# A graph layer and an inverted bottleneck in one kernel: transpose moved up, two images per loop turn, last taps as GpSimd products added by DMA

## The chip, the core and the metric

The kernel runs on one core of a Trainium2 chip. Its engines are TensorE (PE in the profile: matmuls; PEld is its loading of weights), VectorE (DVE), ScalarE (ACT), GpSimd (POOL) and SyncE (SP), which issues DMAs. The engines run their own instruction streams in order and meet through semaphores. The metric is the time of one execution on the device in microseconds; lower is better.

## The reference

The input `x` is 16 images of 96 channels and 64 x 64 pixels, float32. Layer 0 is a graph layer over windows of 8 x 8 pixels; layer 1 is a 1x1 convolution to 576 channels, a depthwise 3x3 convolution and a 1x1 convolution back.

```
y = affine(conv1x1(x, fc1_w, fc1_b), fc1_s, fc1_t)
nodes = windows of y: 64 nodes with 96 features each
idx = the 9 nearest nodes by the distance of normalised features
feat = concatenate([x_i, x_j - x_i])
h = max over the 9 neighbours of gelu(affine(feat @ ew.T + eb))
x = affine(conv1x1(h, fc2_w, fc2_b), fc2_s, fc2_t) + x      # layer 0
h = relu(bn(w1 @ x))                                        # 96 -> 576
h = relu(bn(depthwise 3x3 of h, nine taps per channel))
x = x + bn(w2 @ h)                                          # 576 -> 96
```

## The kernel before

The unit of layer 0 is a pair of windows, 128 nodes; an image has 32 pairs (`p`), 4 to a chunk of 8 rows, and the run has 512 (`P`). The unit of layer 1 is a strip of 16 rows, four to an image, with the 576 channels in four full groups of 128 and a half group (`gr` 0 to 4). One strip is done in the time of 8 pairs; it follows the chunks of layer 0 by two strips. Everything is laid out by hand: for each engine a function `image` runs over the pairs of an image, and its text is the order of the instructions. The images -1, 0, 15 and 16 (starts and ends) are written out, and images 1 to 14 are a hardware loop, one image per turn (`image_loop`).

Within pair `p` the engines do, for layer 0:

- TensorE: `scores` of pair P+3, `gather` part 0 of P, `expand` of P+1 (the one-hot matrix of neighbour offsets, into `pvu`), `feature_transpose` of P+2 (the offsets, transposed into `pself`), `gather` part 1, `self_full`, `values` of P+1 (into `pvu` again), `gather` part 2, `self_half`. Between them stand the shared jobs (`misc_jobs`: fc1, ssq, inv, fc2, w1, w2), which take turns in three banks `pmisc`.
- ScalarE: `gelu` part 0 of P, `onehot` of P+1 (from `pvu` to `MV`), `featT_copy` of P+2, `gelu` part 1, `vu_copy` of P+1 (from `pvu` to `VU`), `feature_square` of P+3, `gelu` part 2, `gelu_self`, with the evacuations of the shared jobs between them; at the pair's end `tap0` and `relu2` of layer 1 where the tables say so.
- VectorE: `largest`, `indices` and `feature_a` of P+3, `maxima` of P-1, and between them the taps.
- GpSimd: the norms, copies of `xn` to `xs`, and two kinds of accumulating DMA (`add_input` and `add_x1`).

Waits that the change touches: `self_full` waits for `featT_evac` of P+2, since both live in one bank; `feature_transpose` waits for `self_gelu` of the pair before it and for `feat_ready`; `values` waits for `onehot_ready`; `gather` part 0 waits for `vu_evac`.

The depthwise convolution of a group is nine taps into `acc`: `tap0` on ScalarE (it writes), taps 1 to 8 on VectorE (multiply and add, `hpad` and `acc` in, `acc` out), then `relu2` on ScalarE and w2 on TensorE. `TAP_AT` gives each of the 8 slots of a strip its taps; a slot `o` falls on pairs with p = o modulo 8. The taps of the half group have 512 columns, the others 1024.

Of the kernel before, what the change touches and what calls it, by code (L numbers as in the profile page):

```python
# [4 lines left out]
B, C, H, W = 16, 96, 64, 64  # L5
# [37 lines left out]
TAP0_LATE = {0: [0], 1: [1], 2: [2], 4: [3]}  # L43
RELU2_AT = {6: [0], 7: [1], 10: [2], 11: [3, 4]}
W2_AT = {12: 0, 13: 1, 14: 2, 16: 3}
TAP_COUNTS = [5, 4, 4, 6, 4, 5, 6, 6]
# [3 lines left out]
FIRST = [(g, k) for k in range(1, TAPS) for g in (0, 1)]  # L50
SECOND = [(g, k) for k in range(1, TAPS) for g in (2, 3, 4)]
# [107 lines left out]
def tap_number(s, g, k):  # L159

    k -= 1
    return s * 5 * (TAPS - 1) + (2 * k + g if g < 2 else 2 * (TAPS - 1) + 3 * k + g - 2) + 1
# [7 lines left out]
def build(nc, x, p97, p128, rows97, consts, consts128, consts16, out):  # L170
# [3 lines left out]
    with ctx:  # L174
# [26 lines left out]
        def col97(k):  # L201
# [45 lines left out]
        acc = sb("acc", [128, 2, 5, STRIP * W])  # L247
        res = sb("res", [C, 2, CW])
# [25 lines left out]
            "vu_ready", "vu_evac", "gather_ready", "self_ready", "gelu_done", "self_gelu"))  # L274
        sp_passed, pool_passed, dve_passed = sem("sp_passed"), sem("pool_passed"), sem("dve_passed")
# [5 lines left out]
        def image_loop(eng, image, tail):  # L281

            image(-1, 16, PAIRS)
            image(0, 0, PAIRS)
            with eng.Fori(1, B - 1) as b:
                image(b, 0, PAIRS)
            image(B - 1, 0, PAIRS)
            image(B, 0, tail)
# [63 lines left out]
        def _(pool):  # L352
# [10 lines left out]

            def add_x1(b, p, o, t, s, q):

                fb, fp = when(b, p, 1)
                pool.wait_ge(misc_evac, job_at(fb, fp, "w2", q))
                pool.sem_inc(pool_passed, 1)
                c = 2 * t + q // 2
                nc.gpsimd.dma_start(res[:, q // 2, :], x1v[:, c * CW:(c + 1) * CW],  # L370
                                    accum_op=ALU.add).then_inc(out_sum[q // 2], 16)
# [33 lines left out]
            def image(b, p0, p1):  # L405
                for p in range(p0, p1):
                    h = 1 if p < 16 else 0
                    bi = b if h else b + 1
                    if p % 16 == NORMS_AT and valid(bi, B):
                        inverse_norms(b, p, bi, h)  # L410
                    for o, t, s, q in due_in(ADD_AT, b, p):
                        add_x1(b, p, o, t, s, q)
                    if p % 16 in XN_AT and valid(bi, B):
                        stationary_copy(bi, 4 * h + XN_AT[p % 16])
                    if p % 4 == 1:
                        bc, c = (b, (p - 5) // 4) if p >= 5 else (b - 1, CHUNKS - 1)
                        if valid(bc, B):
                            add_input(b, p, bc, c)
# [5 lines left out]
        def _(pe):  # L424
# [168 lines left out]
            def image(b, p0, p1):  # L593
                for p in range(p0, p1):
# [7 lines left out]
                    if valid(P, NPAIRS):  # L602
# [4 lines left out]
                        gather(P, p, 0)  # L607
                    for k in part_of(jobs, 0):
                        shared_job(b, p, k, jobs[k])
                    if valid(P + 1, NPAIRS):  # L610
                        expand(P + 1, p + 1)
                    if valid(P + 2, NPAIRS):
                        feature_transpose(P + 2, p + 2)
# [19 lines left out]
        def _(act):  # L633
            def shared_evac(b, p, k, job):
# [37 lines left out]
                elif kind == "w1":  # L672
                    t, s, (gr, m) = job[1:]
                    if m == 0:

                        if due(count := tap_number(s - 1, gr, TAPS - 1)):
                            act.wait_ge(tap_done, count)
                    sc, sh = sc1[:, gr:gr + 1], sh1[:, gr:gr + 1]
# [98 lines left out]
            def relu2(s, par, gr):  # L777
                if due(count := tap_number(s, gr, TAPS - 1)):
                    act.wait_ge(tap_done, count)
# [10 lines left out]
            def image(b, p0, p1):  # L790
                for p in range(p0, p1):
# [7 lines left out]
                    if valid(P, NPAIRS):  # L799
                        gelu(P, p, 0)  # L800
                    for k in part_of(jobs, 0):
# [6 lines left out]
                    if valid(P + 2, NPAIRS):  # L808
                        featT_copy(P + 2, p + 2)
# [255 lines left out]
```

## Time and profile before

| What | Value |
|---|---|
| Median of 3 runs | 4372.47 us (4371.74 to 4379.67) |
| Profiled execution | 4362.46 us |
| Its span | 4360.7 us |
| Mean granted TensorE clock | 0.99 |
| PE busy | 4041.2 us, 26688 matmuls |
| DVE busy | 4081.9 us, 5296 instructions |
| ACT busy | 3606.4 us, 7141 instructions |
| POOL busy | 503.2 us, 548 instructions |

The span is the profiled execution from its first to its last instruction. Busy times are unions, so instructions that overlap by some tens of ns on one engine count once. PE, DVE and ACT overlap almost everywhere, and their order in time is what the rows further down are for.

### The profile page before, as it was taken

Reading aid. Unit: us, or ns where it says so; the run is one execution under the profiler, and the core shown is the slowest. Engines: PE = TensorE matmul, PEld = TensorE weight load, DVE = VectorE, ACT = ScalarE, POOL = GpSimd, SP = SyncE. Lnnn points to the kernel's source line nnn. Section 1 sums busy time; section 2 is a strip of 40 time slices with the busy share of each in tenths; the row PEclk is TensorE's granted clock in tenths of the full one; section 3 lists DMA queues with packets and bytes.
Section 4 is the critical chain, followed back from the end, with each engine's and each line's share of the span. In section 5 each row is a group of like instructions: output and inputs, shape, how many; then the busy total and the mean of one; then the engine's idle time right before and its main releaser. Section 6 shows DMA issues by size and latency. Waiting matters only on the chain.

```text
span 4360.7 us, 84229 instructions
## 1 busy us (share of the span) xinstructions
PE 4041.2 (93%) x26688; PEld 2406.4 (55%) x26688; DVE 4081.9 (94%) x5296; ACT 3606.4 (83%) x7141; POOL 503.2 (12%) x548
## 2 busy tenths in 40 slices
PE   4999999999999999999999999999999999999994
PEld 2555555555555555555555555555555555555552
DVE  2599999999999999999999999999999999999998
ACT  3788888888888888888888888888888888888883
POOL 0011111011111011011111010111010111010100
PEclk9999999999999999999999999999999999999997
DMA  1111120111111111121111111111111111201111
GB/s 47 23 30 32 25 45 18 33 38 32 33 30 28 29 36 34 25 44 19 33 36 33 33 26 24 37 33 33 30 33 25 38 32 25 45 18 25 30 21 24
DMA packets 53036, 134.61 MB, mean 31 GB/s; under 512 B 7778, under 2 KB 9058, under 8 KB 46372
## 3 DMA queue, kind: packets, MB, share of 16 engines
q0 software_dynamic: 28672, 50.35, 8.1%
q1 hardware_dynamic: 23876, 78.22, 6.7%
q8 instruction: 250, 4.10, 0.4%
q14 instruction: 238, 1.95, 0.2%
HBM read 77.68 MB, written 25.69 MB: 24 GB/s over the span
## 4 chain that ended last, share of the span: by engine, by line
PE 66%; issue 11%; DVE 11%; ACT 11%; DMA 0%; SPq 0%; ACTq 0%; DVEq 0%; POOL 0%; POOLq 0%
PE pg L567 15%; PE pmisc L493 8%; PE pg L570 8%; DVE acc L949 8%; PE pvu L554 7%; PE pmisc L477 5%; PE pself L581 5%; ACT MV L741 4%; PE pmisc L438 3%; PE pmisc L460 2%; PE pmisc L462 2%; PE pmisc L445 2%; PE pvu L540 2%; ACT hpad L688 2%; PE pmisc L495 2%
## 5 line engine op out<-in xcount | busy, mean ns | idle before, releaser
L949 DVE SCALAR_TENSOR_TENSOR acc<-hpad,w,acc 128x1024 f32<-128x1024 f32 (+1 forms) x2560 | 2919.5, 1174 | 66.1 <-ACT acc L774 66.1
L567 PE MATMUL pg<-MV,VU 128*128 128x512 f32 x2048 | 1148.0, 643 | 22.6 <-ACT VU L749 21.0
L758 ACT ACTIVATE g<-pg 128x512 f32<-128x512 f32 x1536 | 916.3, 597 | 147.5 <-PE pg L570 90.2
L936 DVE TENSOR_REDUCE hid<-g 128x192 f32<-128x1728 f32 x512 | 995.5, 1944 | 0.0
L741 ACT ACTIVATE MV<-pvu,cst 64x512 f32<-64x512 f32 x1024 | 694.8, 678 | 9.9 <-PE pvu L540 0.3
L477 PE MATMUL pmisc<-x,w 96*128 96x384 f32 (+1 forms) x1536 | 567.9, 481 | 18.4 <-ACT hpad L688 18.4
L570 PE MATMUL pg<-MV,VU 128*64 128x512 f32 x2048 | 530.3, 595 | 0.0
L493 PE MATMUL pmisc<-acc,w 128*96 128x256 f32 x2048 | 492.3, 384 | 31.3 <-ACT acc L781 31.3
L688 ACT ACTIVATE hpad<-pmisc,sh,sc 128x384 f32<-128x384 f32 (+1 forms) x768 | 482.4, 660 | 25.0 <-DVE acc L949 15.7
L477 PEld LDWEIGHTS pmisc<-x,w 96*128 96x128 f32 x1536 | 294.1, 192 | 326.0 <-issue 229.1
L581 PEld LDWEIGHTS pself<-MV,VU 128*128 128x128 f32 x2048 | 283.3, 191 | 335.7 <-issue 314.6
L493 PEld LDWEIGHTS pmisc<-acc,w 128*96 128x96 f32 x2048 | 334.8, 165 | 228.7 <-issue 122.5
L554 PE MATMUL pvu<-wVU,y 97*64 97x192 f32 x4096 | 447.9, 340 | 1.7 <-ACT MV L741 1.7
L581 PE MATMUL pself<-MV,VU 128*128 128x64 f32 x2048 | 308.3, 273 | 141.9 <-ACT featT L727 138.3
L749 ACT ACTIVATE VU<-pvu 128x384 f32<-128x384 f32 x512 | 250.9, 490 | 192.0 <-PE pvu L554 189.4
L781 ACT ACTIVATE acc<-acc,shd,scd 128x1024 f32<-128x1024 f32 (+1 forms) x320 | 358.0, 1142 | 24.4 <-DVE acc L949 24.4
L567 PEld LDWEIGHTS pg<-MV,VU 128*128 128x128 f32 x2048 | 309.4, 191 | 61.2 <-issue 30.4
L774 ACT ACTIVATE acc<-hpad,w 128x1024 f32<-128x1024 f32 (+1 forms) x320 | 334.2, 1044 | 0.0
L587 PEld LDWEIGHTS pself<-MV,VU 128*64 128x64 f32 x2048 | 145.4, 135 | 296.8 <-issue 296.8
L540 PEld LDWEIGHTS pvu<-featT,c 128*128 128x128 f16 x4096 | 186.0, 100 | 181.0 <-issue 156.5
L554 PEld LDWEIGHTS pvu<-wVU,y 97*64 97x64 f32 x4096 | 249.2, 136 | 55.6 <-ACT MV L741 2.0
L403 POOL COPY xs<-xn 96x512 f32<-96x512 f32 x128 | 159.5, 1247 | 1034.1 <-DVE xn L930 1034.1
(95 smaller groups left out, 4125.3 us busy)
## 6 DMA issues: line engine op xcount, KB each, us to landing
xin<-in_x_dram SPq DMA_DIRECT2D x32, 768.0 KB, 5.5
invb<-rows_dram SPq DMA_DIRECT2D x32, 768.0 KB
x<-in_x_dram POOLq DMA_DIRECT2D x128, 192.0 KB, 3.6
res<-x POOLq DMA_DIRECT2D x128, 192.0 KB, 3.6
out_dram<-res SPq DMA_DIRECT2D x128, 192.0 KB, 2.1
g<-in_consts_dram SPq DMA_DIRECT2D x1, 640.0 KB
w<-in_p_dram SPq DMA_DIRECT2D x1, 618.5 KB
rows_dram<-norm_rows SPq DMA_DIRECT2D x32, 16.0 KB, 1.4
```

The lines of the kernel that those rows point to most:

```text
L477: last = nc.tensor.matmul(ps[:, o:o + (hi - lo) * W], w1T[:, gr * 128:(gr + 1) * 128], x1[:, lo:hi, :], start=True, stop=True)
L493: nc.tensor.matmul(ps[0:C, 0:4 * W], w2T[:, gr, :], acc[:, par, gr, q * 4 * W:(q + 1) * 4 * W], start=(gr == 0), stop=False)
L554: last = nc.tensor.matmul(pvu[h:h + 64, O * w:O * (w + 1)], nodes, wVU[:, k, :], start=True, stop=True)
L567: last = nc.tensor.matmul(ps[:, :], VU[:, r, part, 0:ONE128], cols[part], start=True, stop=True)
L570: last = nc.tensor.matmul(ps[64 * w:64 * w + 64, :], VU[:, r, w, ONE128:O], cols[w], start=True, stop=True)
L581: nc.tensor.matmul(pself[:, 64 * w:64 * w + 64], VU[:, r, w, 0:ONE128], MV[:, r, w, KN * NODES:], start=True, stop=True)
L688: nc.scalar.activation(hpad[:, gr, r0:r1, 1:W + 1], ps[:, o:o + (r1 - r0) * W].rearrange("p (row col) -> p row col", col=W), ACT.Relu, bia ...
L741: last = nc.scalar.activation(MV[h:h + 64, p % 2, w, 0:KN * NODES].rearrange("p (n k) -> p n k", k=KN), pone[h:h + 64, :, :].rearrange("p ...
L758: nc.scalar.activation(g[:, p % 2, part, :, 0:KN], pg[(3 * p + part) % 2][:, :].rearrange("p (n k) -> p n k", k=KN), ACT.Gelu).then_inc(ge ...
L781: nc.scalar.activation(acc[:, par, gr, 0:n], acc[:, par, gr, 0:n], ACT.Relu, bias=shd[:, gr:gr + 1], scale=scd[:, gr:gr + 1]).then_inc(rel ...
L936: nc.vector.tensor_reduce(hid[:, c % 2, j, :, :], g[:, r], op=ALU.max, axis=AX.X).then_inc(hid_ready, 1)
L949: nc.vector.scalar_tensor_tensor(out=dst, in0=src, scalar=wk, in1=dst, op0=ALU.mult, op1=ALU.add).then_inc(tap_done, 1)
```

## The change

It has three parts. The transposed offsets: `feature_transpose` of pair P+2 stands directly behind `gather` part 0 on TensorE, and `featT_copy` directly behind `gelu` part 0 on ScalarE. The loop: a turn holds two images, and there are 7 turns. The taps: tap 8 of each of the four full groups leaves VectorE. GpSimd computes it as a product into a new buffer `tapped` (two halves, used in turn), and an accumulating DMA adds it to `acc` once taps 0 to 7 are there. `relu2` of these groups waits for that DMA, and the evacuation that overwrites `hpad` waits for the product too. The taps are spread anew over the slots (36 a strip, before 40), and `tap0` of group 3 moves from slot 4 to slot 3.

```diff
-TAP0_LATE = {0: [0], 1: [1], 2: [2], 4: [3]}
+TAP0_LATE = {0: [0], 1: [1], 2: [2], 3: [3]}
 RELU2_AT = {6: [0], 7: [1], 10: [2], 11: [3, 4]}
 W2_AT = {12: 0, 13: 1, 14: 2, 16: 3}
-TAP_COUNTS = [5, 4, 4, 6, 4, 5, 6, 6]
+TAP_COUNTS = [5, 4, 5, 4, 5, 4, 5, 4]
+PRODUCT_AT = {2: 0, 3: 1, 6: 2, 7: 3}
+SUM_AT = {5: (0, 1), 9: (2, 3)}
...
-FIRST = [(g, k) for k in range(1, TAPS) for g in (0, 1)]
-SECOND = [(g, k) for k in range(1, TAPS) for g in (2, 3, 4)]
+FIRST = [(g, k) for k in range(1, TAPS - 1) for g in (0, 1)]
+SECOND = [(2, 1), (3, 1), (2, 2), (3, 2), (4, 1), (2, 3), (3, 3), (4, 2), (2, 4), (3, 4), (4, 3), (2, 5), (3, 5), (4, 4),
+          (2, 6), (3, 6), (2, 7), (3, 7), (4, 5), (4, 6), (4, 7), (4, 8)]
...
+        tapped = sb("tapped", [128, 2, STRIP * W])
...
-            with eng.Fori(1, B - 1) as b:
+            with eng.Fori(1, B - 2, 2) as b:
                 image(b, 0, PAIRS)
+                image(b + 1, 0, PAIRS)
...
+            def tap_product(b, p, o, s, gr):
+
+                fb, fp = when(b, p, o - w1_slot(gr, 2))
+                pool.wait_ge(misc_evac, job_at(fb, fp, "w1", (gr, 2)))
+                pool.sem_inc(pool_passed, 1)
+                if due(count := 16 * (s if gr < 2 else s + 1)):
+                    pool.wait_ge(tap_sum[(gr + 2) % FULL], count)
+                pool.sem_inc(pool_passed, 1)
+                nc.gpsimd.tensor_scalar(tapped[:, gr % 2, :].rearrange("p (row col) -> p row col", col=W),
+                                        hpad[:, gr, 2:2 + STRIP, 2:2 + W], wd[:, gr, TAPS - 1:TAPS], None,
+                                        ALU.mult).then_inc(product_done, 1)
+
+            def add_product(t, s, gr):
+
+                pool.wait_ge(product_done, FULL * s + gr + 1)
+                pool.sem_inc(pool_passed, 1)
+                pool.wait_ge(tap_done, last_tap(s, gr))
+                pool.sem_inc(pool_passed, 1)
+                nc.gpsimd.dma_start(acc[:, t % 2, gr, :], tapped[:, gr % 2, :],
+                                    accum_op=ALU.add).then_inc(tap_sum[gr], 16)
...
                         gather(P, p, 0)
+                    if valid(P + 2, NPAIRS):
+                        feature_transpose(P + 2, p + 2)
                     for k in part_of(jobs, 0):
                         shared_job(b, p, k, jobs[k])
                     if valid(P + 1, NPAIRS):
                         expand(P + 1, p + 1)
-                    if valid(P + 2, NPAIRS):
-                        feature_transpose(P + 2, p + 2)
...
+                        if gr < FULL and due(count := FULL * (s - 1) + gr + 1):
+                            act.wait_ge(product_done, count)
...
             def relu2(s, par, gr):
-                if due(count := tap_number(s, gr, TAPS - 1)):
-                    act.wait_ge(tap_done, count)
+                if gr < FULL:
+                    act.wait_ge(tap_sum[gr], 16 * (s + 1))
+                else:
+                    act.wait_ge(tap_done, last_tap(s, gr))
...
                         gelu(P, p, 0)
+                    if valid(P + 2, NPAIRS):
+                        featT_copy(P + 2, p + 2)
...
-                    if valid(P + 2, NPAIRS):
-                        featT_copy(P + 2, p + 2)
```

The order on the engines at three places follows; the line numbers of the changed kernel are some 37 to 41 higher for the same instruction.

TensorE in pair 14 of an image in the loop, before: `scores` (pscore), `gather` (pg), the job w2 (acc,w), `expand` (featT,c), the transpose (c,feat), `self_full` (pself from MV,VU) and `values` (wVU,y).

```order
L517 MATMUL pscore<-xn,xs 64x64 x2
L519 MATMUL pscore<-c 64x64 x2
L562 ISA
L567 MATMUL pg<-MV,VU 128x512
L430 REGISTER_ALU
L493 MATMUL pmisc<-acc,w 96x256 x4
L495 MATMUL pmisc<-acc,w 96x256
L540 MATMUL pvu<-featT,c 128x64 x8
L530 MATMUL pself<-c,feat 128x64
L567 MATMUL pg<-MV,VU 128x512
L581 MATMUL pself<-MV,VU 128x64 x2
L554 MATMUL pvu<-wVU,y 64x192 x4
```

The same pair after the change:

```order
L554 MATMUL pscore<-xn,xs 64x64 x2
L556 MATMUL pscore<-c 64x64 x2
L599 ISA
L604 MATMUL pg<-MV,VU 128x512
L567 MATMUL pself<-c,feat 128x64
L467 REGISTER_ALU
L530 MATMUL pmisc<-acc,w 96x256 x4
L532 MATMUL pmisc<-acc,w 96x256
L577 MATMUL pvu<-featT,c 128x64 x8
L604 MATMUL pg<-MV,VU 128x512
L618 MATMUL pself<-MV,VU 128x64 x2
L591 MATMUL pvu<-wVU,y 64x192 x4
```

The transpose has moved from behind `expand` to ahead of the job; the rest keeps its order.

ScalarE at the end of pair 3 (and 11, 19, 27), before: the `VU` copy, the square of `feat`, the last two gelus, and `relu2` (acc from acc) of groups 3 and 4.

```order
L749 ACTIVATE VU<-pvu 128x384
L731 REGISTER_ALU
L732 ACTIVATE feat<-feat 128x16
L753 REGISTER_ALU
L758 ACTIVATE g<-pg 128x64x8
L764 ACTIVATE g<-pself 128x192
L781 ACTIVATE acc<-acc,shd,scd 128x1024
L781 ACTIVATE acc<-acc,shd,scd 128x512
```

The same place after the change:

```order
L788 ACTIVATE VU<-pvu 128x384
L770 REGISTER_ALU
L771 ACTIVATE feat<-feat 128x16
L792 REGISTER_ALU
L797 ACTIVATE g<-pg 128x64x8
L803 ACTIVATE g<-pself 128x192
L813 ACTIVATE acc<-hpad,w 128x1024
L822 ACTIVATE acc<-acc,shd,scd 128x1024
L822 ACTIVATE acc<-acc,shd,scd 128x512
```

`tap0` of group 3 (acc from hpad) now stands ahead of the two `relu2`; it has left the end of the next pair.

GpSimd in pair 1 of an image in the loop, with what each instruction waits for, before: a sum of x1 and the input chunk.

```order
L285 ISA
L370 DMA res<-x 96x512 [waits misc_evac]
L359 REGISTER_ALU
L361 ISA [waits misc_evac]
L361 DMA x<-in_x_dram 96x512
```

The same pair after the change, and the two products of pairs 2 and 3 behind it:

```order
L391 ISA [waits product_done]
L393 DMA acc<-tapped 128x1024 [waits tap_done]
L389 REGISTER_ALU
L391 REGISTER_ALU [waits product_done]
L393 DMA acc<-tapped 128x1024 [waits tap_done]
L399 ISA
L402 DMA res<-x 96x512 [waits misc_evac]
L370 REGISTER_ALU
L372 ISA [waits misc_evac]
L372 DMA x<-in_x_dram 96x512
L381 ISA [waits misc_evac]
L383 TENSOR_SCALAR tapped<-hpad,w 128x1024 [waits tap_sum2]
```

Two sums of products come first, and the two older DMAs queue behind them; the product behind waits until the first of these sums has landed.

## Rows read from the trace of the kernel before

**Rows 1.** The page, busy us, share of the span, instructions

```profile
PE 4041.2 (93%) x26688; PEld 2406.4 (55%) x26688; DVE 4081.9 (94%) x5296; ACT 3606.4 (83%) x7141; POOL 503.2 (12%) x548
```

**Rows 2.** Waits of the whole run: us in total, times, longest us

```profile
ACT VU L749 <- PE pvu L554: 189.4, 248, 1.4
...
PE pself L581 <- ACT featT L727: 138.3, 200, 2.1
...
ACT feat L732 <- DVE feat L919: 32.1, 47, 11.0
...
PE pscore L517 <- issue: 26.3, 13, 2.3
...
PE pmisc L460 <- DVE hid L936: 14.4, 15, 4.1
```

**Rows 3.** Windows: start:end length, busy us by engine, clock, DMA share, GB/s

```profile
1890.21:1956.86 66.65, 65.84 (x440) 39.99 (x438) 63.04 (x82) 58.34 (x117) 7.44 (x10) 1.00 0.19 39
1956.86:2019.95 63.09, 58.79 (x398) 34.80 (x396) 61.72 (x82) 54.18 (x110) 8.31 (x9) 1.00 0.13 24
...
1923.71:1933.84 10.13, 10.13 (x67) 6.58 (x65) 10.13 (x13) 8.05 (x17) 0.92 (x2) 1.00 0.00 0
1979.60:1988.54 8.94, 7.71 (x55) 4.41 (x53) 8.94 (x13) 7.76 (x17) 1.42 (x1) 1.00 0.00 0
...
2118.01:2127.41 9.40, 8.66 (x57) 5.26 (x55) 9.40 (x13) 6.75 (x13) 2.29 (x3) 1.00 0.05 5
```

**Rows 4.** Timeline of pair 14: start us, length us, what, idle time before

```profile
2001.68 1.36 ACT L741 ACTIVATE MV<-pvu,cst 64x512 f32<-64x512 f32 x2
...
2003.07 0.22 ACT L727 ACTIVATE featT<-pself 128x64 f16<-128x64 f32 x1
...
2003.43 0.63 PE L581 MATMUL pself<-MV,VU 128*128 128x64 f32 x4 [0.96 <-ACT featT L727]
...
2003.99 0.87 PE L554 MATMUL pvu<-wVU,y 97*64 97x192 f32 x8
...
2004.92 0.49 ACT L749 ACTIVATE VU<-pvu 128x384 f32<-128x384 f32 x1 [1.14 <-PE pvu L554]
```

**Rows 5.** Waits in the stretch 123 to 181 us, first image, no taps yet

```profile
PE pself L581 <- ACT featT L727: 8.6, 8, 1.2
```

**Rows 6.** Timeline at the start of pair 17

```profile
2021.30 0.52 ACT L764 ACTIVATE g<-pself 128x192 f32<-128x192 f32 x1
...
2021.91 1.02 PE L438 MATMUL pmisc<-xin,w 96*96 96x512 f32 x2
```

**Rows 7.** Timelines of VectorE and GpSimd where copies run

```profile
157.64 0.61 POOL L403 COPY xs<-xn 96x512 f32<-96x512 f32 x1 [5.28 <-DVE xn L930]
157.69 0.58 DVE L919 SCALAR_TENSOR_TENSOR feat<-idx,cst 128x16 f16<-128x16 uint32 x1
...
1977.54 1.28 DVE L949 SCALAR_TENSOR_TENSOR acc<-hpad,w,acc 128x1024 f32<-128x1024 f32 x1
1977.89 1.40 POOL L403 COPY xs<-xn 96x512 f32<-96x512 f32 x1 [14.95 <-DVE xn L930]
1978.74 0.09 DVE L909 MATCH_VALUE_LOAD idx<-top,pscore 128x8 f32 x1
...
2003.18 0.88 POOL L403 COPY xs<-xn 96x512 f32<-96x512 f32 x1 [5.54 <-DVE xn L930]
```

**Rows 8.** Groups by form: count, busy us, mean ns of one, idle before

```profile
L774 ACT ACTIVATE acc<-hpad,w 128x1024 f32<-128x1024 f32 x256 | 287.8, 1124 | 0.0
...
L919 DVE SCALAR_TENSOR_TENSOR feat<-idx,cst 128x16 f16<-128x16 uint32 x512 | 88.0, 172 | 0.7
```

**Rows 9.** The page, DMA: queue's packets, MB, share; issue's KB, us to landing

```profile
q0 software_dynamic: 28672, 50.35, 8.1%
...
res<-x POOLq DMA_DIRECT2D x128, 192.0 KB, 3.6
```

**Rows 10.** Timeline of VectorE at the end

```profile
4246.22 95.18 DVE L949 SCALAR_TENSOR_TENSOR acc<-hpad,w,acc 128x1024 f32<-128x1024 f32 x88
```

More of the change, by code:

```diff
@@ L159, in tap_number, with last_tap @@
 def tap_number(s, g, k):
-    k -= 1
-    return s * 5 * (TAPS - 1) + (2 * k + g if g < 2 else 2 * (TAPS - 1) + 3 * k + g - 2) + 1
+    return s * len(FIRST + SECOND) + (FIRST + SECOND).index((g, k)) + 1
+def last_tap(s, g):
+    return tap_number(s, g, TAPS - 2 if g < FULL else TAPS - 1)
 def due(count):
@@ L274, in build @@
             "vu_ready", "vu_evac", "gather_ready", "self_ready", "gelu_done", "self_gelu"))
+        product_done = sem("product_done")
+        tap_sum = [sem(f"tap_sum{k}") for k in range(FULL)]
         sp_passed, pool_passed, dve_passed = sem("sp_passed"), sem("pool_passed"), sem("dve_passed")
@@ L410, in image @@
                         inverse_norms(b, p, bi, h)
+                    for o, t, s, groups in due_in(SUM_AT, b, p):
+                        for gr in groups:
+                            add_product(t, s, gr)
                     for o, t, s, q in due_in(ADD_AT, b, p):
                         add_x1(b, p, o, t, s, q)
+                    for o, t, s, gr in due_in(PRODUCT_AT, b, p):
+                        tap_product(b, p, o, s, gr)
                     if p % 16 in XN_AT and valid(bi, B):
@@ L674, in shared_evac @@
                     if m == 0:
-                        if due(count := tap_number(s - 1, gr, TAPS - 1)):
+                        if due(count := last_tap(s - 1, gr)):
                             act.wait_ge(tap_done, count)
+                        if gr < FULL and due(count := FULL * (s - 1) + gr + 1):
+                            act.wait_ge(product_done, count)
                     sc, sh = sc1[:, gr:gr + 1], sh1[:, gr:gr + 1]
```

## Prediction

> **What bounds the kernel now.** I read the page first [rows 1]: TensorE is busy for 93% of the span, VectorE for 94% and ScalarE for 83%, so no engine has much room, and the averages can't say which of them the others wait for. The list of waits over the whole run can [rows 2]. Three things stand in it. TensorE waits 138.3 us in `self_full` for ScalarE's copy `featT`, and 26.3 us in 13 turns of the loop. ScalarE waits 189.4 us for `pvu`, which TensorE fills in `values`. And hardly anybody waits for VectorE: ScalarE 32.1 us for `feat` (part of it while the kernel starts), TensorE 14.4 us for `hid`. VectorE is full, but it seldom holds anyone up.
>
> Then I cut one image into pairs, from one `VU` copy to the next, and read the busy time of each stretch [rows 3]. The first line is the strip of pairs 1 to 8, the second that of pairs 9 to 16; the load differs because fc1 and ssq fall on pairs 1 to 6. In the first strip TensorE is busy 65.84 of 66.65 us: it is TensorE's. In the second it is busy 58.79 of 63.09 us, VectorE 61.72. Pair 5 (third line) is TensorE's without a gap, 10.13 of 10.13 us, and leaves ScalarE 2 us of room. Pair 12 (fourth line) takes 8.94 us though TensorE has 7.71 and ScalarE 7.76 of work.
>
> Pair 14 shows the mechanism [rows 4]. The one-hot activation (L741) ends at 2003.04, `featT` (L727) at 2003.29, and only then does `self_full` start, at 2003.43, after 0.96 us of idling; `values` can start at 2003.99, and ScalarE itself idles 1.14 us until `pvu` is full. Both engines stand still in one ring. Where ScalarE doesn't idle before the `VU` copy, the same wait of TensorE costs nothing: ScalarE is then the bound.
>
> **The change part by part.** All sums are made against the profiled execution, 4362.46 us; the median of the runs shown is 10.0 us more, which I add at the end.
>
> *Loop turns.* 14 turns become 7, each with the same work in it twice, so 7 branches back go. Each cost TensorE 26.3 / 13 = 2.02 us [rows 2], with nothing beside it in a pair that is TensorE's: **-14.1 us**. From 0 (if the longer body stalls on its own) to -14.
>
> *Transpose and `featT` early.* `self_full` no longer waits; the ring now closes from the one-hot's end to `values`. The one-hot comes 0.14 us later (TensorE does the transpose first, or ScalarE the copy), and TensorE starts 0.14 us after ScalarE's end as it did at 2003.43: 2003.04 + 0.14 + 0.14 = 2003.32 against 2003.99, so 0.67 us are won where both engines idle. That is in pairs 14 and 30 of each image, 31 in all: **-20.8 us**. In the first image, before the taps begin, almost every pair looks like this (8 waits of about 1.1 us in a stretch of 58 us [rows 5]); some 12 such pairs give **-8.0 us**. In pairs 11, 15, 27 and 31 `self_full` waits too, but ScalarE goes from work to work: 0.
>
> The price lies in `feature_transpose` itself. It waits for `self_gelu` of the pair before, and stands now right behind `gather` 0, where nothing covers it. In [rows 6] that activation (L764) ends at 2021.82, and TensorE goes on behind its gather at 2021.91; with the 0.14 us from above the transpose starts at 2021.96, 0.05 us late. Queued behind it are all of TensorE's jobs of the pair. In about nine of sixteen pairs, those that [rows 3] cut this way show as TensorE's, this is lost: 0.05 x 9 x 32 = **+14.4 us** (from 0 to 0.14 us each, +40).
>
> *`tap0` of group 3 from pair 4 to pair 3.* Seen between `VU` copies, about 1.0 us of ScalarE (L774, 1.12 us [rows 8] less the overlap with its neighbour) moves from the stretch of pair 5, in which it has room, into the stretch of pair 4 (and 12, 20, 28), which holds `relu2` of groups 3 and 4 as well. There the one-hot comes 1.0 us later, and 0.14 us from the edit before. In pair 4 `values` then starts about 0.4 us late, in pair 20 about 0.25; in pair 12 this eats what the early `featT` gives. Over 15 images **+9.8 us** (from 0 to +30).
>
> *Four full taps a strip leave VectorE.* A full tap takes 1.20 us from its start to the next one's (1977.54 to 1978.74 in [rows 7]): 4.8 us of some 62 us a strip. What this is worth is what others wait for VectorE, in the main part of the run in pairs 28 and 29 (9.40 us for 8.66 us of TensorE's work, last line of [rows 3]) and ScalarE's 0.4 us in pair 12, which the moved `tap0` takes: 0.9 x 15 = **-13.5 us**. The bounds are 0 and all waits on VectorE in [rows 2], -46 us.
>
> *The products on GpSimd.* No product of this size stands in the trace; the nearest row is the copy of 96x512 [rows 7]. It took 0.61 us with VectorE quiet (157.64), and 1.40 us when a tap ran as it came. VectorE pays as well: the small `feat` instruction beside the copy took 0.58 us, against a mean of 172 ns [rows 8]. So one holds the other up for as long as it runs. A product has twice the columns: between 0.6 us (no cost per column) and twice the 0.88 us of a half-covered copy (2003.18), 1.76 us; I take 1.1 us, the quiet copy and as much again less its fixed part. It costs VectorE nothing while `maxima` runs (nearly 2 of some 8 us) and up to 1.1 us in a row of taps, so at most 4.4 us of the 4.8 come back as stalls. I cost that at nothing in the body: VectorE then has 61.72 - 4.8 + 4.4 = 61.3 us in the strip of 63.09, and the first two products fall on the pair that keeps only four half taps. The cover is gone at 1.2 us a product.
>
> The Trainium skill has this as a rule (SBUF — State Buffer, "Who interferes with whom"): a VectorE instruction with two SBUF inputs and a GpSimd instruction that reads SBUF exclude each other for the whole instruction. The trace agrees, by 0.58 us against 172 ns. GPSIMD Engine Reference, "Elementwise — side-by-side cycle accounting", gives 1.03 cycles an element where a port is the limit; by it a product would be an estimated 0.9 us, and the sum the same.
>
> *The sums by DMA.* POOL issues 256 transfers more. In 28672 packets the queue's present transfers used 8.1% of the engines; those of 192 KB took 3.6 us to land [rows 9], so I expect 5 to 7 us for 512 KB. `relu2` comes more than ten us after the issue in every slot. Queued behind the sums on POOL are `add_x1`, the input chunk and the next product; the chunk is used two pairs later. Cost 0. Late next, were a sum 20 us under way, would be `relu2` of group 1 and w2 behind it.
>
> *The end.* After the last `maxima` VectorE runs 88 taps in 95.18 us with nobody beside it [rows 10]. After the change there are 77, with 12 full ones fewer and one half more: -13.6 us. Eight products break in, at 0.75 us: +6. The last sum lands about 3 us after the last tap, where now three `relu2` follow at once: +3. **-4.6 us.**
>
> Sum: -14.1 - 20.8 - 8.0 + 14.4 + 9.8 - 13.5 - 4.6 = -36.8; 4362.5 - 36.8 + 10.0 = **4336 us**, 0.8% faster.
>
> **The rivals.**
> 1. *TensorE becomes the only bound.* If my view that ScalarE holds pairs 11, 12 and 15 is wrong, and VectorE does by keeping everything late, then strips shrink to TensorE's busy time, 65.84 and 58.79 us: 5.1 us a pair of strips, 30 of them, -153, with the loop -167: about 4205 us. For it: VectorE's 94%, and 61.72 of 63.09 us. Against it: the short list of waits on VectorE.
> 2. *The product holds VectorE too long, and the kernel is slower.* Place: VectorE's row of taps in pairs 9 to 16. At 1.76 us a product, four cost 7.0 us for 4.8 won, VectorE needs 63.9 us where it needed 61.72, and the 32 such strips lose 2.2 us each, +70; the 13.5 are lost and the end pays 8 more: about 4428 us. It decides from 1.2 us a product.
> 3. *No change.* The transpose waits 0.14 us instead of 0.05: +26, which makes 4362 us; with the moved `tap0` at its upper bound as well, +20 more, 4382 us. The old 4372 lies between. For it: the order only moves a wait within one ring. Against it: in pair 14 both engines of the ring idle.
>
> **How the numbers follow.** Forecast, 20 to 85 us faster: 0.52. Rival 1: 0.18. Rival 3: 0.14. Slower, rival 2 or the upper ends of rival 3: 0.16. A measurement tells some 0.2% (9 us) from nothing, so faster 0.70, same 0.14, slower 0.16. The likeliest case alone spans 4290 to 4352. The range for 8 in 10 leaves out the lower half of rival 1 and the upper half of rival 2: 4245 to 4390.
>
> **What the profile after would show.** Right: no wait of `self_full` on `featT`, instead short ones of the transpose and of `values` on the one-hot; 6 loop waits near 2 us; VectorE's busy share down to 88 to 92%; products near 1.1 us without, 2 us with a tap before them; TensorE about as busy in us as now; pair 4 longer, the start of `values` in pair 14 some 0.7 us earlier in its pair. Wrong: VectorE's share stays at 94% with stretched taps (rival 2); TensorE idles below 2% between images 1 and 14 (rival 1); `relu2` waits on a sum; the second half of a turn stalls for instructions.

## The result and the profile after

The changed kernel took 4389.49 us (median of 6 runs, 4387.09 to 4391.21), the kernel before 4372.10 us beside it (6 runs, 4365.06 to 4379.67). The ratio is 1.0038, with a 95% interval of 1.0026 to 1.0051: 0.38% slower. The forecast was 4336 us; 4389.5 lies just inside the upper end of the range, on the side that was given 16%. The profiled span went from 4360.7 to 4385.9 us.

The page of the changed kernel, as in [rows 1]:

```profile
PE 4098.3 (93%) x26688; PEld 2418.2 (55%) x26688; DVE 3891.9 (89%) x5040; ACT 3623.8 (83%) x7141; POOL 1575.7 (36%) x1060
```

VectorE is 190 us less busy, GpSimd 1072 us more, and TensorE, with the same matmuls, 57 us more. The last is the first sign: a matmul whose weights are still being loaded counts as busy (below, in pair 17, the transpose's record starts at 2026.38, and its weights are in at 2026.45).

The waits of the whole run (us in total, times, longest), beside [rows 2]:

```profile
PEld pself L567 <- issue: 283.8, 448, 1.7
...
ACT VU L788 <- PE pvu L591: 135.2, 224, 1.7
...
PEld pself L567 <- ACT feat L771: 80.5, 64, 2.2
...
ACT feat L771 <- DVE feat L960: 69.2, 81, 11.2
...
PE pvu L591 <- ACT MV L780: 36.9, 92, 1.5
...
PE pscore L554 <- issue: 11.0, 6, 2.1
```

The wait of `self_full` on `featT` (138.3 us) has gone, and the 13 turns are 6. In their place stands a weight load, that of the transpose (L567): TensorE's loader stood idle before it 448 times. And ScalarE waits twice as long for VectorE's `feat`. The strips of image 7, cut as in [rows 3], first strip, second strip, pair 12:

```profile
1892.74:1960.89 68.15, 67.21 (x440) 40.09 (x438) 61.09 (x79) 58.70 (x117) 25.49 (x18) 1.00 0.35 67
1960.89:2024.41 63.52, 59.79 (x398) 35.06 (x396) 58.28 (x78) 54.27 (x109) 22.88 (x16) 1.00 0.30 59
1983.47:1992.99 9.52, 7.26 (x51) 4.13 (x47) 9.52 (x13) 8.71 (x18) 1.48 (x2) 1.00 0.00 0
```

The strip that is TensorE's grew from 66.65 to 68.15 us, the other from 63.09 to 63.52 though VectorE has 3.44 us less work in it. In pair 12 TensorE has work for 7.26 us and the pair takes 9.52 (8.94 before). Pair 14 did what was forecast; the rows that answer to [rows 4]:

```profile
2004.29 0.22 ACT L766 ACTIVATE featT<-pself 128x64 f16<-128x64 f32 x1
...
2006.51 1.37 ACT L780 ACTIVATE MV<-pvu,cst 64x512 f32<-64x512 f32 x2
2007.11 0.56 PE L618 MATMUL pself<-MV,VU 128*128 128x64 f32 x4
...
2007.93 0.87 PE L591 MATMUL pvu<-wVU,y 97*64 97x192 f32 x8 [0.27 <-ACT MV L780]
...
2008.85 0.49 ACT L788 ACTIVATE VU<-pvu 128x384 f32<-128x384 f32 x1 [0.35 <-PE pvu L591]
```

`featT` is ready before the one-hot even starts, and `values` follows the one-hot's end (2007.88) by 0.05 us.

### The profile page after: what moved, and what is told of

The parts are those of the page before. It is cut to its first block, busy times and chain, and to the rows that moved or that the text cites. A ratio compares the mean times of both kernels' runs of the same rounds, so it can differ in the third digit from the quotient of the medians.

```text
span 4385.9 us, 86104 instructions
## 1 busy us (share of the span) xinstructions
PE 4098.3 (93%) x26688; PEld 2418.2 (55%) x26688; DVE 3891.9 (89%) x5040; ACT 3623.8 (83%) x7141; POOL 1575.7 (36%) x1060
## 3 DMA queue, kind: packets, MB, share of 16 engines
q0 software_dynamic: 65536, 184.58, 23.8%
## 4 chain that ended last, share of the span: by engine, by line
PE 63%; ACT 14%; issue 12%; DVE 8%; DMA 1%; SPq 0%; DVEq 0%; ACTq 0%; POOL 0%; POOLq 0%
PE pg L604 15%; PE pmisc L530 8%; PE pg L607 7%; PE pvu L591 7%; PE pmisc L514 7%; DVE acc L990 6%; ACT MV L780 4%; PE pmisc L497 3%; PE pself L618 3%; PE pmisc L482 3%; PE pmisc L499 2%; PE pmisc L475 2%; PE pmisc L532 2%; ACT hpad L727 2%; ACT acc L822 2%
## 5 line engine op out<-in xcount | busy, mean ns | idle before, releaser
L990 DVE SCALAR_TENSOR_TENSOR acc<-hpad,w,acc 128x1024 f32<-128x1024 f32 (+1 forms) x2304 | 2726.2, 1208 | 244.3 <-ACT acc L813 241.7
L383 POOL TENSOR_SCALAR tapped<-hpad,w 128x1024 f32<-128x1024 f32 x256 | 831.1, 3318 | 10.5 <-DMA acc<-tapped 7.1
L393 POOL DMA_DIRECT2D acc<-tapped x256 | 229.6, 898 | 1534.9 <-DVE acc L990 1467.3
L514 PE MATMUL pmisc<-x,w 96*128 96x384 f32 (+1 forms) x1536 | 580.4, 490 | 17.3 <-ACT hpad L727 12.8
L727 ACT ACTIVATE hpad<-pmisc,sh,sc 128x384 f32<-128x384 f32 (+1 forms) x768 | 485.1, 663 | 15.9 <-POOL tapped L383 8.3
L514 PEld LDWEIGHTS pmisc<-x,w 96*128 96x128 f32 x1536 | 280.1, 191 | 260.0 <-issue 161.2
L435 POOL COPY xs<-xn 96x512 f32<-96x512 f32 x128 | 175.6, 1372 | 585.8 <-DVE xn L971 585.8
L618 PEld LDWEIGHTS pself<-MV,VU 128*128 128x128 f32 x2048 | 304.6, 191 | 116.9 <-issue 54.1
```

Source lines behind the costliest of these rows:

```text
L383: nc.gpsimd.tensor_scalar(tapped[:, gr % 2, :].rearrange("p (row col) -> p row col", col=W), hpad[:, gr, 2:2 + STRIP, 2:2 + W], wd[:, gr, ...
L514: last = nc.tensor.matmul(ps[:, o:o + (hi - lo) * W], w1T[:, gr * 128:(gr + 1) * 128], x1[:, lo:hi, :], start=True, stop=True)
L727: nc.scalar.activation(hpad[:, gr, r0:r1, 1:W + 1], ps[:, o:o + (r1 - r0) * W].rearrange("p (row col) -> p row col", col=W), ACT.Relu, bia ...
L990: nc.vector.scalar_tensor_tensor(out=dst, in0=src, scalar=wk, in1=dst, op0=ALU.mult, op1=ALU.add).then_inc(tap_done, 1)
```

## The experiments

The runs fall into three groups, each with its own runs of the kernel before (13, 13 and 10; medians 4367.28, 4367.18 and 4371.52 us); every ratio is to those of its group. Kernels of different groups are best compared by their ratios.

### The three parts one at a time

**Transpose and `featT` early, alone.** The kernel before with the move below in TensorE's `image`, and that of `featT_copy` to behind `gelu` 0 in ScalarE's, as in the change:

```diff
+                    if valid(P + 2, NPAIRS):
+                        feature_transpose(P + 2, p + 2)
                     for k in part_of(jobs, 0):
...
                         expand(P + 1, p + 1)
-                    if valid(P + 2, NPAIRS):
-                        feature_transpose(P + 2, p + 2)
```

> The kernel before with the transpose and the featT copy moved up, and nothing else. What I now hold (A): it wins 0.7 us in pairs 14 and 30 and 8 us in the first image, and loses 0.2 to 0.25 us in every pair that is TensorE's, because the weights of the transpose can't be loaded under the gather: all in all within 15 us of the kernel before, 4357 to 4380. The forecast on record: -14 us. Rival (B), the transpose is what made the change slower: 15 us or more slower than before.

Measured: 4383.20 us, ratio 1.0034 (1.0021 to 1.0047). Slower by itself, by 15.9 us: outside the 4357 to 4380 us of A, and at the near edge of B.

**Two images per turn, alone:**

```diff
-            with eng.Fori(1, B - 1) as b:
+            with eng.Fori(1, B - 2, 2) as b:
                 image(b, 0, PAIRS)
+                image(b + 1, 0, PAIRS)
```

> The kernel before with two images to a loop turn, and nothing else. Forecast and A: 7 waits of about 2 us fewer, 12 to 17 us faster. Rival: the longer body stalls on its own, within 5 us of before.

Measured: 4352.26 us, 0.9963 (0.9950 to 0.9976): 15.0 us faster, where 14.1 were forecast.

**Products, sums, tables and the moved `tap0`, alone:** the changed kernel with those two parts undone.

> The kernel before with the products on GpSimd, their sums by DMA, the new tap tables and tap0 of group 3 a slot earlier. Forecast on record: 8 us faster. A, by what is left when the two other parts are taken off the measured change: 30 to 45 us slower, with about 8 of it after the last pair. B: within 10 us of before.

Measured: 4431.77 us, 1.0150 (1.0132 to 1.0168). The dearest part, at +64.5 us, and more than either expectation had.

**Both order changes, all taps as before:** the change without its third part.

> Transpose moved up and two images a turn, all nine taps as before. A: the sum of the two single runs, 15 to 30 us faster than before. B: slower than before or the same.

Measured: 4352.27 us, 0.9968 (0.9956 to 0.9980). The effects alone add up to -15.0 + 15.9 = +0.9 us, together they are -15.0; all three alone add up to +65, together they are +17. So the parts interact, and each must be read in the pairs, not only in its total; a good part of the interaction may be the granted clock, as the last section estimates.

### Which part of the third part

**Only `tap0` of group 3 moved** (the kernel before, one number):

```diff
-TAP0_LATE = {0: [0], 1: [1], 2: [2], 4: [3]}
+TAP0_LATE = {0: [0], 1: [1], 2: [2], 3: [3]}
```

> The kernel before with tap0 of group 3 at the end of pair 3 (11, 19, 27) instead of 4, and nothing else. Theory A, the moved tap0 is what makes the tap part slow: ScalarE is the bound in these stretches, so each is 0.8 to 1.2 us longer and nothing comes back, 40 to 60 us slower than before. Rival C, the products that hold VectorE are what makes it slow: within 15 us of before. The forecast on record had +10 us.

Measured: 4422.14 us, 1.0132 (1.0115 to 1.0148): +55.0 us for one activation moved by one pair. Products, sums and tables are worth only the other +8 of the +65.

ScalarE and TensorE in pair 4 of that kernel:

```profile
1936.93 1.15 ACT L774 ACTIVATE acc<-hpad,w 128x1024 f32<-128x1024 f32 x1
1937.95 1.96 ACT L781 ACTIVATE acc<-acc,shd,scd 128x1024 f32<-128x1024 f32 x2
...
1941.61 1.36 ACT L741 ACTIVATE MV<-pvu,cst 64x512 f32<-64x512 f32 x2
1943.00 0.22 ACT L727 ACTIVATE featT<-pself 128x64 f16<-128x64 f32 x1
...
1943.37 0.63 PE L581 MATMUL pself<-MV,VU 128*128 128x64 f32 x4 [0.74 <-ACT featT L727]
```

The same two places in the kernel before:

```profile
1922.31 0.55 PE L581 MATMUL pself<-MV,VU 128*128 128x64 f32 x4
...
1923.71 0.49 ACT L749 ACTIVATE VU<-pvu 128x384 f32<-128x384 f32 x1 [0.20 <-PE pvu L554]
```

In the kernel before, too, ScalarE idled only once between the `VU` copy of 1915.53 and that of 1923.71: the 0.20 us of the last line. One more activation of 1.02 us from start to start makes the pair 0.97 us longer. Pair 5, where it came from, is TensorE's and stays at 10.12 us.

**`tap0` back, in the changed kernel** (the same line, the other way round).

> The changed kernel with tap0 of group 3 back at the end of pair 4, and nothing else. A: 30 to 50 us faster than the changed kernel, 4335 to 4355, with pairs 4 and 20 back at 8.4 us. C: within 10 us of the changed kernel's 4389; VectorE now waits for that tap0 in slot 5.

Measured: 4379.20 us, 1.0025 (1.0015 to 1.0035): against 1.0038 only 0.13% or some 6 us of the 55 come back, as C had it and not A. The lengths of the pairs (table below) show why: pairs 4, 12, 20 and 28 lose their 0.7 to 1.0 us each again, but 5, 13, 15, 16, 21, 29 and 0 grow by 0.3 to 0.8 (20, 21 and 28 aren't in the table).

**Tiny products.** The changed kernel, each product over 16 columns. It leaves out all but 16 columns of tap 8 of groups 0 to 3; the sums still move 512 KB, the rest of `tapped` being zero.

```diff
-                nc.gpsimd.tensor_scalar(tapped[:, gr % 2, :]..., hpad[:, gr, 2:2 + STRIP, 2:2 + W], ...)
+                nc.gpsimd.tensor_scalar(tapped[:, gr % 2, 0:16], hpad[:, gr, 2, 2:18], ...)
```

> The changed kernel with products of 16 columns instead of 1024 (most of tap 8 is left out; the sums by DMA stay as they are), so GpSimd hardly touches VectorE's port. C: 30 us or more faster than the changed kernel, 4360 or less. A: only the end (some 10 to 15 us, where the products waited behind the row of taps) and what ScalarE waits for feat in pairs 12, 16, 28, 31 and 0, some 0.7 us each: 4350 to 4375.

Measured: 4352.47 us, 0.9966 (0.9952 to 0.9979): by the two ratios the products' size costs 0.72% or 31 us (38 us by the two spans), 14.6 us of it behind the last `VU` copy (136.2 to 121.6 us).

### Where the transpose stands

**Transpose and copy behind the first jobs.** The kernel before with two images per turn, and the transpose one place earlier than before, not two:

```diff
                     for k in part_of(jobs, 0):
                         shared_job(b, p, k, jobs[k])
+                    if valid(P + 2, NPAIRS):
+                        feature_transpose(P + 2, p + 2)
                     if valid(P + 1, NPAIRS):
                         expand(P + 1, p + 1)
-                    if valid(P + 2, NPAIRS):
-                        feature_transpose(P + 2, p + 2)
```

and on ScalarE `featT_copy` directly ahead of `onehot`. All taps as before.

> Two images a turn, all nine taps as before, and the transpose directly ahead of expand, behind the first of the shared jobs, with the featT copy directly ahead of the one-hot. If the transposes cost comes from its weights, which can't be loaded under the gather while it waits for gelu_self, it is free here, since that wait is long over: 10 us or more faster than the same kernel with the transpose right behind the gather (4352), and pairs 1, 2, 6, 9 as long as before. If the cost lies in the order of the types (float16 between float32) or in the longer way to the one-hot, it stays: within 5 us of 4352.

Measured: 4299.93 us (4298.48 to 4301.96), 0.9845 (0.9831 to 0.9858). It is 52 us below the kernel with both moves early, and faster than both kernels of this study; nothing is left out of it. TensorE's busy time, 4041.2 us before and 4084.8 us with both early, is 4016.7 us.

**Which engine's move it was.** TensorE transposes right behind `gather` 0, as in the change; ScalarE copies late.

> Two images a turn, all taps as before; TensorE transposes right behind gather 0 as in the changed kernel, but ScalarE copies featT late, directly ahead of the one-hot. Theory (the transpose stands where its weight load is not covered, 0.2 us in each pair that is TensorE's): no better than the kernel with both early, 4352 us, range 4345 to 4360. Rival (the early copy on ScalarE ahead of the jobs' activations is what costs): like the kernel with both in the middle, 4300 us, 4295 to 4308. A value between 4310 and 4340 would share it between the two.

Measured: 4358.31 us, 0.9969 (0.9957 to 0.9981): as with both early. The place on TensorE costs the 52 us; that on ScalarE makes no difference that these runs show.

The start of pair 17 in the changed kernel, as [rows 6]:

```profile
2025.41 1.12 PE L604 MATMUL pg<-MV,VU 128*128 128x512 f32 x2
2025.76 0.52 ACT L803 ACTIVATE g<-pself 128x192 f32<-128x192 f32 x1
2026.35 0.10 PEld L567 LDWEIGHTS pself<-c,feat 128*128 128x128 f16 x1 [0.64 <-issue]
2026.38 0.19 PE L567 MATMUL pself<-c,feat 128*128 128x64 f16 x1
2026.57 0.24 PEld L475 LDWEIGHTS pmisc<-xin,w 96*96 96x96 f32 x2
2026.58 1.09 PE L475 MATMUL pmisc<-xin,w 96*96 96x512 f32 x2
```

and with the transpose behind the jobs:

```profile
1987.47 1.12 PE L568 MATMUL pg<-MV,VU 128*128 128x512 f32 x2
...
1988.01 0.16 PEld L439 LDWEIGHTS pmisc<-xin,w 96*96 96x96 f32 x1 [0.24 <-issue]
...
1988.87 0.10 PEld L531 LDWEIGHTS pself<-c,feat 128*128 128x128 f16 x1 [0.27 <-issue]
...
1989.30 0.19 PE L531 MATMUL pself<-c,feat 128*128 128x64 f16 x1
...
1989.33 0.39 PE L541 MATMUL pvu<-featT,c 128*128 128x64 f16 x8
```

Below, each matmul's weights were loaded while the one before it ran (1988.01 for 1988.43, 1988.87 for 1989.30), and the transpose takes 0.03 us from its start to the next one's. Above, it waits for `gelu_self` (2025.76 + 0.52 = 2026.28), its weights are loaded only then, and the job's weights behind it too: 0.20 us from start to start, and the job itself 0.07 us longer. By itself the transpose started on time: 0.97 us behind its gather, where the job started 0.96 us behind it before. Medians over 14 images of the kernel with both early say that the wait makes the difference: with the same job behind, a sum of squares, the transpose takes 0.20 us in pairs 2, 5, 6, 18, 21 and 22, where it starts 0.10 us behind the end of `gelu_self` (it waited), and 0.10 us in pairs 3 and 19, where it starts 0.20 us behind (it didn't). In pairs 11 and 16, with a w1 job behind it, it starts 0.19 to 0.20 us behind and takes 0.03 us. The wait isn't the whole account: in pairs 4 and 20 it did wait and takes 0.11 us ahead of fc1, where it takes 0.20 us in pairs 1 and 17; why is open. The other suspect, a float16 instruction between float32 ones, finds no support: in the kernel before, the float32 gather behind the transpose starts 0.03 us after it (2023.00 and 2023.03).

### The order that works, with products

**The changed kernel with the transpose and copy behind the jobs** (the order of the experiment above, in the changed kernel).

> The changed kernel with the transpose and the featT copy moved behind the first part of the pair's jobs; tap0, products and sums stay. If the price of the transpose is separate from the rest: 4389 - 52 = 4337 us, range 4325 to 4350, faster than before. Rival, VectorE held by products and the moved tap0 bound the changed kernel, so that a shorter ring on TensorE is worth little: 4370 to 4390 us.

Measured: 4325.10 us, 0.9896 (0.9881 to 0.9911): 1.4% below the changed kernel.

**And `tap0` of group 3 back in pair 4.**

> The kernel of the run before this one, with tap0 of group 3 back in pair 4; products and sums stay. It stands against the kernel with all taps on VectorE and the same order, 4300 us, and shows what products and sums are worth alone. Theory (each product takes about as much from VectorE as the tap gave, and the end is longer by 8 to 15 us): 4310 to 4330 us. Rival (VectorE is now the late one in pairs 13, 15, 29 and 31, so that four taps less a strip pay): 4260 to 4295 us.

Measured: 4308.84 us, 0.9853 (0.9838 to 0.9868), against 0.9845 without products and sums; just under the range of the theory (4310 to 4330 us), and far from the rival's. What the products take from VectorE's shorter work and from the end is just what the four taps gave; which of the two kernels is the better one the intervals can't tell.

**And tiny products in it** (leaves out what the first such kernel did).

> The kernel of the run before this one with products of 16 columns in place of 1024 (this leaves out tap 8 of groups 0 to 3, all but 16 columns of it); the sums by DMA stay. It shows what a product at no cost would give. If VectorE is late next in that order: 4265 to 4285 us, 15 to 35 below 4300. If the taps are hidden anyway, only the end gives: 4290 to 4300 us. The distance to the run with full products is their whole price, 15 us of it at the end as read before.

Measured: 4272.21 us, 0.9770 (0.9757 to 0.9783). Full products cost 36.6 us, and taking tap 8 off VectorE at next to no price would be worth 0.75% (0.9845 to 0.9770).

What a product does to a half tap in pair 14, with the full product:

```profile
1976.96 1.97 DVE L990 SCALAR_TENSOR_TENSOR acc<-hpad,w,acc 128x512 f32<-128x512 f32 x1
1977.28 2.83 POOL L383 TENSOR_SCALAR tapped<-hpad,w 128x1024 f32<-128x1024 f32 x1
1978.85 0.16 DVE L960 SCALAR_TENSOR_TENSOR feat<-idx,cst 128x16 f16<-128x16 uint32 x1
...
1979.05 0.21 ACT L771 ACTIVATE feat<-feat 128x16 f16<-128x16 f16 x1 [0.71 <-DVE feat L960]
```

and with the tiny one:

```profile
1961.01 0.88 DVE L991 SCALAR_TENSOR_TENSOR acc<-hpad,w,acc 128x512 f32<-128x512 f32 x1
1961.33 0.76 POOL L383 TENSOR_SCALAR tapped<-hpad,w 128x16 f32<-128x16 f32 x1
```

The half tap takes 1.09 us more, `feat` comes late by as much, and ScalarE waits 0.71 us for it. `maxima` (1.94 us) runs beside the rest of the product and is no longer for it.

### The pairs side by side

Lengths from one `VU` copy to the next in us, means over images 1 to 14, worked out from each trace (the means include pairs in which the granted clock fell, pair 0 above all; "early": two images per turn and both moves; "behind": two images per turn and the transpose behind the jobs):

| Pair | before | tap0 moved | early | changed | changed, tap0 back | behind | behind, products | behind, tiny products |
|---|---|---|---|---|---|---|---|---|
| 4 | 8.19 | 9.16 | 8.44 | 9.12 | 8.44 | 8.19 | 8.19 | 8.18 |
| 5 | 10.12 | 10.12 | 10.40 | 10.05 | 10.39 | 10.12 | 10.12 | 10.12 |
| 12 | 8.98 | 10.16 | 8.47 | 9.53 | 8.51 | 8.61 | 8.64 | 8.62 |
| 13 | 8.45 | 8.45 | 8.99 | 8.65 | 9.00 | 8.89 | 8.90 | 8.90 |
| 14 | 7.93 | 7.94 | 7.22 | 7.22 | 7.21 | 7.14 | 7.14 | 7.14 |
| 15 | 7.12 | 7.13 | 7.62 | 7.13 | 7.52 | 7.68 | 7.56 | 7.12 |
| 16 | 7.91 | 7.91 | 7.74 | 8.43 | 8.74 | 7.65 | 8.07 | 7.65 |
| 29 | 9.34 | 8.45 | 9.52 | 8.77 | 9.53 | 9.84 | 9.84 | 9.84 |
| 0 | 10.58 | 10.74 | 8.97 | 9.55 | 10.10 | 8.73 | 9.57 | 8.83 |
| all 32 | 262.89 | 266.47 | 262.68 | 264.80 | 264.65 | 259.15 | 260.16 | 258.07 |

## Why the prediction was wrong

**Loop turns: right.** -14.1 forecast, -15.0 measured alone.

**Transpose and `featT` early, the gain: right.** Pairs 14 and 30 became 0.71 us shorter (0.67 forecast), and the first image, from its first `VU` copy to the 33rd, went from 230.6 to 220.5 us (8.0 forecast, 10.1 measured). The forecast of nothing in pairs 11, 15, 27 and 31 didn't quite hold: 11 and 27 gain 0.3 us, and 15 and 31 lose 0.5 us. VectorE comes late there once the pairs ahead are shorter: with the order "behind", pair 15 takes 7.68 us with all taps and 7.12 us with tiny products.

**The price of the transpose: the step that failed by mechanism.** The prediction asked when the transpose could start, found it 0.05 us late, and priced that at +14.4. The start came a little sooner than that, 0.01 us late. What it missed is that the weight loads behind the waiting instruction stand still too: pairs 1, 2, 4, 5, 6, 9, 21, 22 and 25 are 0.16 to 0.34 us longer with the early order than before, three to seven times what was priced, and with the transpose behind the jobs 52 us come back. With 0.25 instead of 0.05 the term is +72, the old sum +21, and 4393 us, 4 us from the result. That closeness is partly chance: the moved `tap0`, the taps, the products and the end were off as well, some up and some down.

**Moved `tap0`, +9.8: mis-sized, +55.0 alone.** The prediction let the one-hot come 1 us late and granted the ring 0.6 us of slack in pair 4. ScalarE had 0.20 us in the whole pair, and in pairs 12, 20 and 28 it passes on all of it: +0.97, +1.18 (1.03 where the clock stayed), +1.05 and +1.04 us an image, and -0.89 in pair 29, where ScalarE's relief helps. In the changed kernel undoing it gives only 6 us, and with the transposes behind the jobs 16 us (4325.10 to 4308.84): pairs 13 and 29 grow again by 0.5 and 1.0 us there. In pair 29 of that order it is VectorE that comes late, as the rows below show. Why pair 5 gives back 0.3 us too was not tested.

**Four taps leave VectorE, -13.5: too small.** At hardly any price for the product they give 0.75% or 33 us (0.9770 against 0.9845), 3.5 us of it behind the last `VU` copy (129.1 to 125.6 us). Once the transposes are out of the way, VectorE is what comes late: in pair 29 of the kernel with them behind the jobs,

```profile
2084.97 0.21 ACT L733 ACTIVATE feat<-feat 128x16 f16<-128x16 f16 x1 [0.83 <-DVE feat L920]
...
2086.95 1.07 PE L461 MATMUL pmisc<-hid,w 128*96 128x256 f32 x4 [1.17 <-DVE hid L937]
```

**Products on GpSimd cost nothing in the body: failed.** 1.1 us was forecast for one; by form, the products and the taps of the changed kernel:

```profile
L990 DVE SCALAR_TENSOR_TENSOR acc<-hpad,w,acc 128x1024 f32<-128x1024 f32 x1792 | 2328.2, 1318 | 241.7 <-ACT acc L813 241.7
L383 POOL TENSOR_SCALAR tapped<-hpad,w 128x1024 f32<-128x1024 f32 x256 | 831.1, 3318 | 10.5 <-DMA acc<-tapped 7.1 <-issue 2.5
L990 DVE SCALAR_TENSOR_TENSOR acc<-hpad,w,acc 128x512 f32<-128x512 f32 x512 | 419.8, 820 | 2.6
```

A product takes 3.3 us in the mean, three times the forecast: the copy of 96x512 was a poor stand-in for a multiplication of 128x1024. But it doesn't hold VectorE for as long as it runs, which is how [rows 7] were read: the half tap lost 1.1 us to a product of 2.83 us, and the rest went on beside `maxima`. Over the run VectorE is 99 us busier than with tiny products (3891.9 against 3792.5 us), which is 0.4 us for each of 256; a full tap takes 1318 ns in the mean against 1282 before, a half one 820 against 741. So rival 2 named the right mechanism with the wrong price of either side: no 2.2 us a strip, but 27 us over the body (36.6 less 9.3 at the end, transposes behind the jobs; they lie in pairs 0, 15, 16 and 31, at 0.4 to 0.7 us each), in the main through the one instruction that matters, `feat` (ScalarE's wait for it is 56.8 us with tiny products and 99.5 us with full ones).

**Sums by DMA, 0: right in the body.** The page's issues (KB, us from issue to landing): 

```profile
acc<-tapped POOLq DMA_DIRECT2D x256, 512.0 KB, 4.8
...
res<-x POOLq DMA_DIRECT2D x128, 192.0 KB, 5.4
```

A sum lands in 4.8 us (5 to 7 forecast), the queue's share rose from 8.1% to 23.8%, and before the last strips nobody waited for one but GpSimd itself, once, for 1.0 us.

**The end, -4.6: failed, +8.0** (last `VU` copy to the last instruction, 128.2 to 136.2 us). The products were to break into VectorE's row of taps at 0.75 us each. It was mostly the other way round, VectorE's taps held up the products:

```profile
4272.19 82.05 DVE L990 SCALAR_TENSOR_TENSOR acc<-hpad,w,acc 128x1024 f32<-128x1024 f32 x71 [2.38 <-ACT acc L813]
...
4292.95 21.60 POOL L383 TENSOR_SCALAR tapped<-hpad,w 128x1024 f32<-128x1024 f32 x2 [1.95 <-DMA acc<-tapped]
...
4319.34 7.62 POOL L383 TENSOR_SCALAR tapped<-hpad,w 128x1024 f32<-128x1024 f32 x2 [2.19 <-DMA acc<-tapped]
...
4335.36 21.59 POOL L383 TENSOR_SCALAR tapped<-hpad,w 128x1024 f32<-128x1024 f32 x2 [1.98 <-DMA acc<-tapped]
...
4356.91 1.80 POOL L393 DMA_DIRECT2D acc<-tapped  x2
```

ScalarE's timeline behind them:

```profile
4361.57 1.24 ACT L822 ACTIVATE acc<-acc,shd,scd 128x1024 f32<-128x1024 f32 x1 [21.73 <-DMA acc<-tapped]
4364.64 1.95 ACT L822 ACTIVATE acc<-acc,shd,scd 128x1024 f32<-128x1024 f32 x2 [1.83 <-DMA acc<-tapped]
```

VectorE's row of taps runs from 4272.19 to 4354.24. The two products of 4335.36 took 21.6 us and were done 2.7 us after the row; only then could the last sums, `relu2` and w2 follow. But the end of the row isn't what lets a product in: those of 4292.95 took 21.6 us too and were done in the middle of it, and those between took 7.62 us. At 4292.95 and at 4335.36 alike the first of the two took 18.5 us. For some 16 us of them the taps went round groups 2, 3 and 4, none longer than 1.28 us, so it got nowhere; it went on where the last taps of the half group follow each other, and there a tap is stretched:

```profile
4308.78 1.49 DVE L990 SCALAR_TENSOR_TENSOR acc<-hpad,w,acc 128x512 f32<-128x512 f32 x1
```

It isn't the product's size either: in the changed kernel with tiny products the last two of these, of 16 columns, took 16.76 us. Why one order of taps shuts a product out and another doesn't stays open. With tiny products the end is 6.6 us shorter than before.

The other rivals: TensorE never became the only bound (rival 1; even with tiny products in the best order a kernel takes 4272 us, not 4205). Rival 3's lower case, that the transpose loses 0.14 us a pair, went the right way and not far enough.

By the Trainium skill (GPSIMD Engine Reference, "Elementwise — side-by-side cycle accounting") a product was an estimated 0.9 us; the trace shows 2.83 us at the least and 3.12 us in the median of the 256, so here the measurement decides. The sum didn't rest on that figure, it came from the copy, which misled it by as much. By the Trainium skill (SBUF — State Buffer, "Who interferes with whom") the ports that the two engines share are an exclusive lock. That fits the end, where a product got nowhere for 16 us beside a row of taps; it doesn't fit the half tap. That began 0.32 us before the product, and still it lost time, and what it lost was 1.1 us and not 2.83.

## What to carry to other kernels

Before an instruction is moved to where "nothing covers it", look not only at when it can start but at what is preloaded behind it: in this kernel a wait in front of a short matmul also stopped the weight loads of the next. Put such a wait behind a long matmul, here the jobs: with two images per turn the early place was worth 0 us (4352.26 to 4352.27), the place one further down 52 us. Work put on an engine whose pair has no idle time cost its whole length here, 0.97 of 1.02 us. And work given to GpSimd wasn't free for VectorE: beside a tap it lengthened the tap, and in the row of taps at the kernel's end it came late itself.

## What the runs showed of the hardware

**A product of 128x1024 against one of 128x16.** In pair 14 it takes 2.83 against 0.76 us; over all 256, with the transposes behind the jobs, the medians are 3.13 and 0.61 us. So 1008 columns more cost 2.1 to 2.5 us. In the row of taps at the end the longest took 18.5 us, and 16.0 us with 16 columns.

**A loop turn costs more than its 2.0 us of waiting in some turns.** In the kernel before, pair 0 takes 8.02 us without a turn, about 10.3 us with most, and 11.7 to 12.3 us with four. Windows of one of those four (turn into image 10; PEclk is the third figure from the end):

```profile
2670.20:2672.40 2.20, 0.00 (x0) 0.00 (x0) 2.20 (x3) 1.83 (x3) 0.00 (x0) 1.00 0.04 11
2672.40:2674.00 1.60, 1.56 (x9) 0.92 (x10) 1.60 (x4) 0.00 (x0) 0.00 (x0) 0.98 0.04 10
2674.00:2676.00 2.00, 2.00 (x12) 1.12 (x11) 2.00 (x6) 1.46 (x3) 0.00 (x0) 0.50 0.02 4
2676.00:2677.10 1.10, 1.10 (x2) 0.34 (x1) 1.10 (x2) 1.06 (x3) 0.00 (x0) 0.50 0.00 0
2677.10:2679.00 1.90, 1.90 (x9) 1.33 (x8) 1.90 (x3) 1.49 (x3) 0.00 (x0) 0.94 0.00 0
```

TensorE stood still for 2.33 us, went on at the granted clock 1.00, and some 1.6 us later, busy nearly all of them, fell to 0.50 (1.2 of 2.4 GHz) for 3.4 us, which costs an estimated half of that: pair 0 takes 11.7 to 12.3 us with such a fall and about 10.3 without. By the granted clock over the two pairs at each turn this happened in 4 of 13 turns of the kernel before, in 11 of 13 with the transpose early and one image per turn, in 4 of 6 with two images per turn alone, in none of 6 with both, and in 1 of 6 of the changed kernel.

**The clock falls away from the turns too.** Up to the last `VU` copy the profiled executions have these stretches at 0.50, nearly all of them 3.4 us long:

| Kernel | falls | us at 0.50 | span, us |
|---|---|---|---|
| before | 7 | 24 | 4360.7 |
| transpose early, alone | 11 | 38 | 4384.6 |
| two images per turn, alone | 17 | 65 | 4352.8 |
| both ("early") | 0 | 0 | 4348.0 |
| `tap0` moved, alone | 15 | 51 | 4414.5 |
| third part alone | 19 | 72 | 4430.5 |
| changed | 1 | 3 | 4385.9 |

At half of each as an estimate, the early transpose alone paid 7 us more than the kernel before, two images per turn alone 20 us more, and both together 12 us less. That is enough for the 29 us by which the first two parts miss adding up in the spans (+23.9 and -7.9 against -12.7), and it says that some 14 of the 54 us of the moved `tap0` may be the clock as well. These are estimates from one execution each, but the mean granted clocks of the other runs lie the same way: 0.991 to 0.992 with both, 0.983 to 0.991 for the kernel before beside it, whose run at 0.991 took 4358.75 us and that at 0.983 took 4378.51 us. What decides a fall stays open.
